# The fourth product with v leaves its bank in one copy and is split by GpSimd, which also takes the remainders of the rows and of the context

## The reference

```python
h = _layernorm(x, ln1_g, ln1_b)
x = _attention(h, h, sa_wq, sa_wk, sa_wv, sa_wo, sa_bo) + x
h = _layernorm(x, ln2_g, ln2_b)
x = _attention(h, cond_emb, ca_wq, ca_wk, ca_wv, ca_wo, ca_bo) + x
h = _layernorm(x, ln3_g, ln3_b)
p = h @ ff_w1 + ff_b1
a, gate = (p[..., :D_FF], p[..., D_FF:])
h = a * jax.nn.gelu(gate, approximate=False) @ ff_w2 + ff_b2
return h + x
```

## Time and profile before

| | |
|---|---|
| median of 3 runs | 2842.57 us (2842.28 to 2843.34) |
| the profiled execution, its own time | 2842.41 us |
| its span in the profile | 2840.6 us |
| granted clock of PE over the span | 0.999 |
| PE busy | 2796.0 us (98%) |
| DVE busy | 2262.0 us (80%) |
| ACT busy | 1910.5 us (67%) |
| POOL busy | 1468.7 us (52%) |

### The profile page before, as it was taken

One profiled execution on the slowest core, in us unless ns is written; L12 is line 12 of the kernel. 1 busy time (PEld: TensorE's weight loads), 2 busy tenths in 40 slices (PEclk: granted clock), 3 DMA queues, 4 the chain that ended last, 5 costly groups with the idle time before them and its releaser, 6 DMA issues.

```text
span 2840.6 us, 72796 instructions
## 1 busy us (share of the span) xinstructions
PE 2796.0 (98%) x25278; PEld 2490.1 (88%) x25278; DVE 2262.0 (80%) x3494; ACT 1910.5 (67%) x6043; POOL 1468.7 (52%) x1311
## 2 busy tenths in 40 slices
PE   8999999999999999999999999999999999999999
PEld 7888888888888888888888888888888889999999
DVE  7888888888888888888888888888888865555554
ACT  6777777777777777877777777777777754444443
POOL 5444444444444444755555555555555564554554
PEclk9999999999999999999999999999999999999999
DMA  6666666666666666767777776666666642222222
GB/s 158 151 160 161 162 161 162 162 154 153 155 153 153 151 153 153 179 166 173 172 173 172 171 171 164 164 164 164 165 164 163 149 101 86 80 74 82 84 74 64
DMA packets 355330, 413.33 MB, mean 146 GB/s; under 512 B 122017, under 2 KB 209441, under 8 KB 355233
## 3 DMA queue, kind: packets, MB, share of 16 engines
q1 hardware_dynamic: 345088, 395.29, 57.2%
q10 hardware_dynamic: 10144, 16.78, 1.6%
HBM read 94.52 MB, written 49.02 MB: 51 GB/s over the span
## 4 chain that ended last, share of the span: by engine, by line
PE 58%; issue 17%; POOL 12%; DVE 11%; ACT 1%; POOLq 0%; DMA 0%; DVEq 0%; ACTq 0%
PE unit_ps L629 31%; PE s_ps L629 12%; POOL probs L1357 10%; PE unit_ps L653 8%; PE s_ps L641 7%; DVE neg_max L1107 3%; DVE blocks L1121 2%; DVE hT_lo L1145 2%; DVE qk L1132 1%; POOL x_rb L1344 1%; ACT probs L911 1%; DVE row_blocks L1098 1%; POOL rstd L1336 1%; DVE a_lo L1127 0%; DVE hT_lo L1149 0%
## 5 line engine op out<-in xcount | busy, mean ns | idle before, releaser
L1357 POOL TENSOR_TENSOR probs<-probs,row_inv 128x1024 f32<-128x1024 f32 x512 | 972.6, 1900 | 1076.5 <-DVE row_inv L1112 1076.4
L911 ACT ACTIVATE probs<-s_ps,neg_max 128x256 f32<-128x256 f32 x2048 | 950.2, 486 | 508.7 <-DVE neg_max L1107 507.7
L1121 DVE STREAM_TRANSPOSE blocks<-probs 128x1024 f32<-128x1024 f32 x512 | 633.2, 1237 | 194.6 <-POOL probs L1357 194.6
L1107 DVE TENSOR_REDUCE neg_max<-s_ps 128x4 f32<-128x1024 f32 x512 | 611.5, 1195 | 5.6 <-PE s_ps L641 2.7
L629 PE MATMUL unit_ps<-hT_hi,w_hi 128*128 128x256 f32 x2048 | 580.0, 287 | 5.6 <-DVE hT_lo L1145 3.1
L629 PE MATMUL unit_ps<-hT_hi,w_lo 128*128 128x256 f32 x2048 | 555.1, 277 | 0.0
L629 PE MATMUL unit_ps<-hT_lo,w_hi 128*128 128x256 f32 x1792 | 497.3, 278 | 0.0
L653 PE MATMUL unit_ps<-pT,v_f 128*64 128x256 f32 x4096 | 456.6, 381 | 0.2 <-issue 0.2
L911 ACT ACTIVATION_READ_ACCUMULATOR probs<-s_ps,neg_max 128x1 f32 x2048 | 442.0, 216 | 0.0
L641 PEld LDWEIGHTS s_ps<-qk 64*128 64x128 f32 x6144 | 374.9, 185 | 70.6 <-issue 42.0
L641 PE MATMUL s_ps<-qk 64*128 64x256 f32 x6144 | 426.6, 284 | 5.9 <-ACT probs L911 5.4
(11 more groups left out here) (76 smaller groups left out, 4866.0 us busy)
## 6 DMA issues: line engine op xcount, KB each, us to landing
pT<-blocks SPq DMA_DIRECT2D x1024, 256.0 KB, 4.5
rows_t_dram<-row_blocks SPq DMA_DIRECT2D x91, 256.0 KB, 2.2
rows_in<-rows_t_dram SPq DMA_DIRECT2D x91, 256.0 KB, 4.4
x_res<-in_x_dram SPq DMA_DIRECT2D x32, 256.0 KB, 3.1
x_sa_dram<-x_out SPq DMA_DIRECT2D x32, 256.0 KB, 2.2
x_ln<-x_sa_dram ACTq DMA_DIRECT2D x32, 256.0 KB, 4.9
ctx_in<-in_ctx_dram SPq DMA_DIRECT2D x32, 256.0 KB, 4.1
x_res<-x_sa_dram SPq DMA_DIRECT2D x32, 256.0 KB, 2.8
```

Source lines behind the costliest of these rows:

```text
L911: op = nc.scalar.activation(probs[:, m % 2, r, :].rearrange("p (j b c) -> p j b c", j=IT, c=BLK), scored.rearrange("p (j c b) -> p j b c", ...
L1107: nc.vector.tensor_reduce(neg_max[:, m % RING, :], s_ps[:, m % 2, :, :].rearrange("p h (i j) -> p (h i) j", j=S), AX_X, ALU.max, negate=Tr ...
L1121: nc.vector.transpose(blocks[:, n % 2, :, m % 2, :].rearrange("p b (j r c) -> p r j b c", j=IT, c=BLK), probs[:, m % 2, :, :].rearrange("p ...
L1357: nc.gpsimd.tensor_tensor(probs[:, m % 2, :, :], probs[:, m % 2, :, :], row_inv[:, m % RING, :].unsqueeze(2).broadcast_to([P, ROWS, S]), A ...
```

## The change

ACT no longer casts the fourth product with v but copies it whole into a new tensor `a_last` (`attended_out`), and that frees the bank. POOL then makes both parts from it: the high part by adding zero, the low part by subtracting (`attended_last`, in step 2 ahead of `normalise` of pair 4). `residual` moves from step 2 to the beginning of step 1 on POOL. In cross-attention `x_remainder` and `context_remainder` move from DVE to POOL, behind `normalise` of pair 5 in step 2. In `end_attention` the fourth product's split moves from DVE to POOL too, ahead of the split of w2. The counts that others wait for are adapted.

```diff
@@ bank_free
+                    elif kind == "a" and rest[0] == STEPS - 1:
+                        at_least(eng, self.a_last_out, b + 1)
                     elif kind == "a":
-                        at_least(eng, self.a_lo_done, b * STEPS + rest[0] + 1)
+                        at_least(eng, self.a_lo_done, b * (STEPS - 1) + rest[0] + 1)
@@ tensor, project_out
-                    pe.wait_ge(at.a_lo_done, b * STEPS + 2 * half + 2)
+                    pe.wait_ge(at.a_lo_done, b * (STEPS - 1) + half + 2)
+                    if half:
+                        pe.wait_ge(at.a_last_lo, b + 1)
@@ scalar
+            def attended_out(b):
+                act.wait_ge(at.o_full, (b + 1) * STEPS)
+                at_least(act, at.a_last_lo, b)
+                nc.scalar.copy(a_last[:], attended_bank(b, STEPS - 1).rearrange("p (i s) -> p i s", i=2)
+                               ).then_inc(at.a_last_out, 1)
@@ scalar, end_attention
-                attended_hi(last, 3)
+                attended_out(last)
@@ scalar, attention_iteration
-                        for k in range(1, STEPS):
-                            attended_hi(t - 1, k)
+                        attended_hi(t - 1, 1)
+                        attended_hi(t - 1, 2)
+                        attended_out(t - 1)
@@ vector, end_attention
-                attended_lo(last, 3)
@@ vector, attention_iteration
-                    if n == 3 and to_context:
-                        context_remainder(t + 1)
-                    if n == 2 and "prv" in parts:
-                        attended_lo(t - 1, 3)
-                    if n == 2 and "nxt" in parts and in_context:
-                        x_remainder(t + 1)
@@ gpsimd
             def context_remainders(b):
                 c = b - ca.first
-                pool.wait_ge(at.norm_done, (b - 1) * PAIRS + 6)
                 pool.wait_ge(at.ctx_hi, c + 1)
+                nc.gpsimd.tensor_tensor(hT_lo[:, 1, 0, :], ctx_in[:, 0, :], f32(hT_hi[:, 1, 0, :]), ALU.subtract).then_inc(at.ctx_lo, 1)
+                pool.wait_ge(at.ctx_lo, 2 * c + 1)
                 nc.gpsimd.tensor_tensor(hT_hi[RIGHT, 1, 1, :], ctx_in[RIGHT, 1, :], f32(hT_hi[RIGHT, 1, 1, :]),
                                         ALU.subtract).then_inc(at.ctx_lo, 1)
                 pool.wait_ge(at.ctx_lo, 2 * c + 2)
+            def x_remainder(b):
+                pool.wait_ge(at.x_hi, b + 1)
+                nc.gpsimd.tensor_tensor(hT_lo[:, 0, :, :], hT[:], f32(hT_hi[:, 0, :, :]), ALU.subtract).then_inc(at.x_lo, 1)
+            def attended_last(b):
+                pool.wait_ge(at.a_last_out, b + 1)
+                at_least(pool, at.wo_full, 2 * b)
+                nc.gpsimd.tensor_tensor(a_hi[:, PAIRS - 2:PAIRS, :], a_last[:], zero[:, 0:1].unsqueeze(2).broadcast_to([P, 2, S]),
+                                        ALU.add).then_inc(at.a_last_hi, 1)
+                pool.wait_ge(at.a_last_hi, b + 1)
+                nc.gpsimd.tensor_tensor(a_lo[:, PAIRS - 2:PAIRS, :], a_last[:], f32(a_hi[:, PAIRS - 2:PAIRS, :]),
+                                        ALU.subtract).then_inc(at.a_last_lo, 1)
@@ gpsimd, end_attention
                 pool.wait_ge(ff_hi_done, 3)
+                attended_last(TOTAL - 1)
                 nc.gpsimd.tensor_tensor(ff_w2_lo, w_stage[:, 2, :], f32(ff_w2_hi), ALU.subtract).then_inc(ff_w2_split, 1)
@@ gpsimd, attention_iteration
+                    if "prv" in parts and n == 1:
+                        residual(at, t - 1, pass_of(t - 1, home).norm)
                     if "prv" in parts and n == 2:
-                        residual(at, t - 1, pass_of(t - 1, home).norm)
+                        attended_last(t - 1)
                     if "cur" in parts:
                         normalise(t, 2 * n)
...
                     if "cur" in parts:
                         normalise(t, 2 * n + 1)
+                    if n == 2 and "nxt" in parts and parts != FILL and pass_of(t, home).has_ctx:
+                        x_remainder(t + 1)
                     if n == 2 and "nxt" in parts and pass_of(t + 1, home).has_ctx:
                         context_remainders(t + 1)
```

More of the change, by code:

```diff
@@ L249, in block_kernel @@
         table = sb("table", [P, IT])
+        a_last = sb("a_last", [P, 2, S])
         PARAMS = 16 * 8
@@ L318, in __init__ @@
                 self.a_lo_done = sem(f"{name}_a_lo_done")
+                self.a_last_out = sem(f"{name}_a_last_out")
+                self.a_last_hi = sem(f"{name}_a_last_hi")
+                self.a_last_lo = sem(f"{name}_a_last_lo")
                 self.wo_full = sem(f"{name}_wo_full")
@@ L1125, in attended_lo @@
             def attended_lo(b, n):
-                dve.wait_ge(at.a_hi_done, b * STEPS + n + 1)
+                dve.wait_ge(at.a_hi_done, b * (STEPS - 1) + n + 1)
                 nc.vector.tensor_tensor(a_lo[:, 2 * n:2 * n + 2, :], attended_bank(b, n).rearrange("p (i s) -> p i s", i=2),
@@ L1145, in x_remainder @@
                 nc.vector.tensor_tensor(hT_lo[:, 0, :, :], hT[:], f32(hT_hi[:, 0, :, :]), ALU.subtract).then_inc(at.x_lo, 1)
-            def context_remainder(b):
-                dve.wait_ge(at.ctx_hi, b - ca.first + 1)
-                nc.vector.tensor_tensor(hT_lo[:, 1, 0, :], ctx_in[:, 0, :], f32(hT_hi[:, 1, 0, :]), ALU.subtract).then_inc(at.ctx_lo, 1)
             def project_out(b, half):
@@ L1218, in attention_iteration @@
                 in_context = parts != FILL and pass_of(t, home).has_ctx
-                to_context = "nxt" in parts and pass_of(t + 1, home).has_ctx
                 for n in range(STEPS):
```

## The result

The changed kernel takes 2863.93 us (median of 4 runs, 2860.85 to 2866.45) against 2842.66 (2842.28 to 2843.34) for the kernel before: a ratio of 1.0074, 95% interval 1.0057 to 1.0091. It is slower. The profiled execution took 2865.61 us, its span is 2863.8, 23.2 more than before.

The account below looks back on a forecast made before the run. It took cross-attention's chain round DVE and POOL, from pair 0's maxima to the next, 35.29 us a period, as the bound. On 2842.41 us, + 9.3 + 2.7 + 4.1 - 0.3 = 15.8 gave 2858 us, range 2845 to 2868.

Parts of the forecast that it names:

- Part 1: ACT's copy of the fourth product frees bank 2 some 5 us earlier; PE's 0.78 us wait goes, gaining nothing by itself.
- Part 2: POOL's split of the fourth product, 2.66 us, fits its 3.28 us hole ahead of `normalise` of pair 4; costs nothing.
- Part 3: Rows' remainder on POOL behind `normalise` of pair 5 makes `queries` late: 35.59 us a cross-attention period, 0.30 more; +9.3 us.
- Part 4: Context's remainders on POOL end 1.7 to 2.0 us after the rows' remainder, just hidden behind `queries`; costs nothing.
- Part 5: At t = 32 and 33 weight splits fill POOL's hole, so the product's split comes 1.4 us late each: +2.7 us.
- Part 6: At attention's end POOL's product split delays w2's split and what follows: +4.1 us; t = 63's removed bank wait returns 0.3.
- A: Rival: rows' remainder not late, PE bounds cross-attention at 34.42 us a period, 27 us won, 6.5 lost: 2822; chance 0.11.
- B: Rival: the rows' remainder's delay is just absorbed, only the losses at t = 32, 33 and end remain: 2846 to 2849; 0.12.
- C: Rival: POOL's new instructions run slower than their rows, or context's remainders come late for PE: 2863 to 2870; chance 0.14.

Follow-up runs that it names:

- product_only: Changed kernel's fourth-product edit alone, on the kernel before; both cross-attention remainders stay on DVE: 2853.73 us, ratio 1.0036.
- context_only: Kernel before with only the context's first remainder moved from DVE to POOL: 2834.81 us, ratio 0.9968.
- remainders_only: Kernel before with both cross-attention remainders on POOL; the fourth product stays with ACT and DVE: 2853.47 us, ratio 1.0036.
- ctx_early_x: Kernel before with the context's first remainder on POOL and the rows' remainder on DVE ahead of the inverse of pair 5: 2825.15 us, ratio 0.9932.
- in_the_middle: whole_early_x with the fourth product split the old way by ACT and DVE for batches 0, 30, 31, 32 and 63: 2823.18 us, ratio 0.9927.
- x_first: Changed kernel with POOL taking the rows' remainder ahead of `normalise` of pair 5 instead of behind it: 2843.55 us, ratio 0.9999.
- whole_early_x: Changed kernel with the rows' remainder on DVE, ahead of the inverse of pair 5: 2832.88 us, ratio 0.9962.
- again: The changed kernel, unaltered, timed once more beside the follow-up kernels: 2867.14 us, ratio 1.0082.
- x_late: Changed kernel with the rows' remainder on DVE at t = 32 and 33 alone: 2866.12 us, ratio 1.0080.
- end_undone: Changed kernel with the last batch's fourth product split by ACT and DVE in `end_attention`, as before: 2864.74 us, ratio 1.0074.
- x_back: Changed kernel with the rows' remainder back at its old place on DVE: 2846.98 us, ratio 1.0013.

## Why the prediction was right

**Part 1, the bank freed early: nothing. Shown.** product_only has no bank wait and the period of before.

**Part 2, POOL's split in its hole: nothing in the period. Shown**, with 1.04 us for the addition where 1.29 was taken: the two start and end within 2.42 us. The two sizes agree otherwise, 1.30 for the subtraction against 1.29. What this part missed is the edges. At the start and at t = 31 POOL has no hole of 3.28 us, since it splits weights there too, and in after that cost 1.9 us in t = 1 and 1.25 in t = 31, where the prediction had none. POOL's timeline in t = 1 of the kernel after, and DVE's transposition that waits for its end:

```profile
70.05 2.41 POOL L1355 TENSOR_TENSOR w_lo<-w_stage,w_hi 128x1024 fp32r<-128x1024 f32 x1
72.41 1.04 POOL L1381 TENSOR_TENSOR a_hi<-a_last,zero 128x512 fp32r<-128x512 f32 x1
73.53 1.29 POOL L1384 TENSOR_TENSOR a_lo<-a_last,a_hi 128x512 fp32r<-128x512 f32 x1
74.78 1.89 POOL L1360 TENSOR_TENSOR probs<-probs,row_inv 128x1024 f32<-128x1024 f32 x1
```

```profile
76.71 1.25 DVE L1136 STREAM_TRANSPOSE blocks<-probs 128x1024 f32<-128x1024 f32 x1 [3.40 <-POOL probs L1360]
```

Iteration t = 1 (from its first maxima to those of t = 2) takes 38.47 us before. The four kernels that don't split on POOL there (context_only, remainders_only, ctx_early_x, in_the_middle) take 38.42 to 38.47, all that do lose: product_only, x_first, whole_early_x and again 1.2 to 1.35 us, and after, x_late, end_undone and x_back, whose granted clock was halved for 3.4 us near 79 or 80, 1.9 to 2.1. A further 1.3 or 1.4 us at the start, in context_only, x_back and again, lie ahead of t = 1 and have nothing to do with the split: in these three profiles the first maxima of t = 1 come at 52.9 to 53.0 us instead of 51.5 to 51.6, and the first stretch at half clock near 39 us instead of near 30. For t = 31 the prediction said that self-attention's slack takes it. Every kernel with POOL's split there lost 1.0 to 1.3 us, and every one without it lost none.

**Part 3, the rows' remainder behind `normalise` of pair 5: 35.59 us a period. Shown**, step by step: 24.64 us unchanged, 1.85 against 1.86, 1.27 against 1.29, 7.69 against 6.69 + 1.01 = 7.70, and 35.50 in sum against 35.59. The difference is the signal to PE, for which 0.10 was allowed and 0.05 is seen (1772.46 + 1.27 to 1773.78). The prediction put +8.7 us on the 29 periods t = 34 to 62; after has +7.6, the other profiles of this code 7.0 to 10.1. x_first turns the cause around: with the remainder ahead of `normalise` the loss of the 29 periods (7.6 us) becomes a gain of 7.5, and the turn costs 1.0 instead of 8.9.

The Trainium skill, GPSIMD Engine Reference, section 4.1, has GpSimd some 2 times slower than VectorE for such work. The rows give 1.27 against 0.69, or 1.84; on the other hand DVE's 0.69 was 2.02 at the old place. Both the place and the engine count. With the rest of the change the same, the period is 35.51 us with the remainder on POOL behind `normalise` (after), 34.98 on DVE at the old place (x_back), 34.99 on POOL ahead of `normalise` (x_first) and 34.62 on DVE ahead of the inverse (whole_early_x).

The Trainium skill, SBUF — State Buffer, "Who interferes with whom", by which the DVE instruction waits for the whole of POOL's, is borne out by ctx_early_x: 0.69 us where POOL isn't scaling, 2.02 where it is.

**Part 4, the context's remainders: nothing. Right for this kernel.** They take 0.73 us each, for which 0.65 to 0.98 and 0.98 were taken, and PE waits for them nowhere in cross-attention's periods. x_first shows how thin the cover is: it is gone as soon as the rows' remainder is early.

**Part 5, POOL without a hole at t = 32 and 33: +2.7 us. Mis-sized.** This is the step that failed. With part 3's 0.6 for these two iterations, 3.3 us were forecast; after lost 7.7, the other kernels with this code 4.8 and 5.0. In POOL's timeline at t = 32 of the kernel after the split, the product's two parts and `normalise` of pair 4 stand back to back, as forecast:

```profile
1187.93 2.40 POOL L1355 TENSOR_TENSOR w_lo<-w_stage,w_hi 128x1024 fp32r<-128x1024 f32 x1
1190.29 1.04 POOL L1381 TENSOR_TENSOR a_hi<-a_last,zero 128x512 fp32r<-128x512 f32 x1
1191.41 1.30 POOL L1384 TENSOR_TENSOR a_lo<-a_last,a_hi 128x512 fp32r<-128x512 f32 x1
1192.67 1.89 POOL L1360 TENSOR_TENSOR probs<-probs,row_inv 128x1024 f32<-128x1024 f32 x1
...
1197.83 1.27 POOL L1376 TENSOR_TENSOR hT_lo<-hT,hT_hi 128x512 fp32r<-128x512 f32 x1
```

```profile
1196.53 0.96 PE L647 MATMUL s_ps<-qk 64*128 64x256 f32 x12 [0.92 <-DVE qk L1147]
1199.24 0.55 PE L635 MATMUL unit_ps<-hT_hi,w_hi 128*128 128x256 f32 x1 [1.75 <-POOL hT_lo L1376]
```

PE waits 0.92 and 1.75 us here within some 3 us, where a steady period has one wait of 1.19, and during the second wait its granted clock halves, from 1198.6 to 1205.4 (0.50 in the window above, that is 1.2 instead of 2.4 GHz). This is what the prediction did not see: it left the granted clock at full speed throughout, a term put at nothing without a reason. PE's own rows give its price. In the stretch at t = 33 the products of `queries` begin 0.213 us apart, behind it 0.113 to 0.12:

```profile
1241.89 0.41 PE L635 MATMUL unit_ps<-hT_hi,w_lo 128*128 128x256 f32 x1
1242.10 0.41 PE L635 MATMUL unit_ps<-hT_hi,w_hi 128*128 128x256 f32 x1
...
1243.57 0.28 PE L635 MATMUL unit_ps<-hT_lo,w_hi 128*128 128x256 f32 x1
1243.68 0.28 PE L635 MATMUL unit_ps<-hT_hi,w_lo 128*128 128x256 f32 x1
```

At this pace 3.4 us hold 16 products instead of 30, so one such stretch costs up to 1.6 us. The three profiles with the same code here (after, again, end_undone) agree. Their waits of PE in these iterations are the same within 0.02 us (0.92 and 1.75 at t = 32, 0.77 and 1.75 at t = 33), but their stretches of 3.4 us at half clock are not, and the loss of an iteration goes with them: with none (t = 33 of again and end_undone) 1.76 and 1.72 us, with one 3.12 to 3.23, with two (t = 32 of after, 6.8 us in a row) 4.53. So each stretch cost 1.4 us here. What is left without them is 1.7 us an iteration, and 1.65 was forecast: the delay on POOL was sized rightly, and after's three stretches, 4.2 us, are what was missed.

It doesn't take both edits: product_only and x_back, with the product's split on POOL and the remainder at its old place on DVE, both lose 5.0 us in the two iterations, with one stretch in each. x_late loses 2.54 and 2.48 with one in each, 0.6 less than the code of after with one; its second wait of PE is 1.06 us instead of 1.75. Where either is missing, the split on POOL or a late remainder (on POOL behind `normalise` or on DVE at the old place), no stretch at half clock followed: x_first and whole_early_x, with the split and an early remainder, lose -0.2 and 1.1 us, remainders_only, without the split, 0.7. That the waits lower the clock is not shown, only that each stretch here stands at one; again and end_undone have the same two waits at t = 33 and keep their full clock.

**Part 6, the end: +4.1 us, less 0.3. Shown** by the rows above and by end_undone. The last stretch lost 4.5 us, PE's three waits are 4.02 (4.1 forecast, though with the first of them 1.72 instead of 1.9), undoing the part gives back 5.0 in end_undone, and 5.5 between whole_early_x and in_the_middle. Kernels without the split there still differ by 2 us in this stretch (-0.5 to +1.6), for which no run has a cause.

**The sum.** Forecast 15.8 us; profiled 23.2. Of the 7.4 between them, 4.4 are part 5 at t = 32 and 33, 1.25 t = 31, 2.2 self-attention from the start on, 0.7 the end, and -1.1 the periods. The median is 2863.93, 21.3 above that of before, 5.9 above the forecast, and 0.9 above the band of 2850 to 2863 that had most of the chance: the path that sets the period was right, and what was short are the edges of the loops.

**The rivals.** A, that PE becomes the bound, did not happen to this change; it needs the rows' remainder off the end of POOL's chain. in_the_middle has PE full at 2823 us, where A gave 2822, but that is luck: A had 27 us won in the periods and 6.5 lost in parts 5 and 6, in_the_middle won 17.5 in the 29 periods and 1.8 at the turn, and lost nothing at the end. B is refuted by the 35.50 us. C's price (2863 to 2870) holds the result, but not its cause: the new instructions ran as fast as their rows or faster, and `keys` waited for nothing.

Still open: why the clock was halved at some of these waits and not at the same ones in other executions, and what the executions of one kernel differ by outside these stretches.

## What to carry to other kernels

A wait that an engine shows is worth its time only if it lies on the chain that sets the period: follow the chain from one instruction to its own next repetition, and then ask of a moved instruction what it stands behind in its new queue. Here standing ahead of or behind one instruction was worth 20 us on POOL (x_first against after) and 10 to 14 on DVE (ctx_early_x against context_only, whole_early_x against x_back), as much as the choice of the engine: DVE instead of POOL was worth 17 us behind (x_back against after) and 11 ahead (whole_early_x against x_first). Cost an edit that fills an engine's idle hole again where that hole is not there, at the start, the turn and the end: product_only lost all its 11.8 us there and none in the steady state.

## What the hardware showed unexpectedly

**Half clock after waits of PE.** The trace of before has the granted clock at 0.5 only once, for 6.8 us near 30 us. The changed kernel has it four times: 3.4 us at 31.3, 3.4 at 79.0, 6.8 at 1198.6 and 3.4 at 1239.6. Each of the last three lies in an iteration where POOL splits a weight piece and PE has just waited, or still waits, longer than in a steady period: 2.01 us at 79 us (the row below), 0.92 and 1.75 at 1198.6, where the clock fell 0.6 us before the second wait ended, 0.77 and 1.75 ahead of 1239.6.

```profile
78.65 0.78 PE L732 MATMUL unit_ps<-ident,x_n 128*128 128x128 f32 x4 [2.01 <-DVE qk L1147]
```

The kernels whose rows' remainder is early have none after the first 40 us, and remainders_only and context_only neither. So a delay of 1 or 2 us on POOL can be followed by half a clock on PE, worth another 1.4 us per 3.4 us of it at the turn and 0.7 at t = 1 (between the two groups of kernels under part 2). It need not be: product_only, whole_early_x and again wait 2.00 or 2.01 us at t = 1 too and keep their full clock there.

**Two paces of the same products.** At a granted clock of 1.00 PE's products follow each other at 0.113 us in some stretches and at 0.118 in others, so that from `queries` to the next scores it is 6.69 or 6.91 us. That gives the periods of two lengths: 35.53 and 35.75 in remainders_only, 35.52 and 35.75 in again, 34.60 and 34.84 in in_the_middle. It moves from run to run (after has mostly the shorter), and 0.22 us in every other period would be the 3 us by which equal code differs in the 29 periods (7.0 to 10.1). No run here shows its cause.
